# A cross-attention block on one core: q earlier and in halves, zero and constant rows by other queues

## The chip, the cores and the metric

The kernel runs on one NeuronCore of a Trainium2 chip. Its engines are TensorE (PE, matmul), VectorE (DVE), ScalarE (ACT), GpSimd (POOL) and SyncE (SP, which here only issues transfers). Two queues of DMAs are used, SP's (SPq, q1) and ACT's (ACTq, q10); their transfers run on the same 16 DMA engines. The metric is the time of one execution on the device in microseconds, lower is better, as the median of several runs. The profile is of one more execution; its times are counted from the start of its span.

## The reference

```python
# x [8,256,256], ctx [8,1601,256], mask all ones; D=256, H=16 heads of HD=16, INNER=1024
residual = hidden_states
x = layer_norm(hidden_states, ln1_w, ln1_b)
q = (x @ q_w + q_b)                      # by heads
k = (encoder_hidden_states @ k_w + k_b)  # by heads
v = (encoder_hidden_states @ v_w + v_b)  # by heads
scores = jnp.einsum('bhqd,bhkd->bhqk', q, k) * scale
scores = jnp.where(mask, scores, mask_value)
attn = jax.nn.softmax(scores, axis=-1)
out = jnp.einsum('bhqk,bhkd->bhqd', attn, v) ... @ cproj_w + cproj_b
hidden = out + residual
y = layer_norm(hidden, ln2_w, ln2_b)
y = gelu(y @ fc_w + fc_b) @ proj_w + proj_b
return hidden + y
```

## The kernel before

Each of the 8 batches has 256 queries and 1601 keys, padded to 13 key tiles of 128 (KT). The order of work is written out by hand, engine by engine, and every dependence is a semaphore.

Products that need full precision are done with each operand split in two parts, high and low, and three matmuls. The context of a batch arrives transposed in four chunks (cT, by `load_ctx`); ACT (in batch 0, `high`) or POOL (later, `c_high`) makes the high part c_hi, and POOL's `c_low` the low part c_lo. From these PE makes K in eight units, `k_unit(b, mt, c)`: mt is one of two groups of eight heads, c the chunk, six matmuls into the bank KB. DVE takes a unit out with two instructions (`k_evac`: kpart, high and low), and SP stores it in DRAM (`store_k`, k_scr). V is made in 13 units of six matmuls (`v_unit`) into the one bank XB, and DVE takes each out with one instruction (`v_evac`). The q path uses XB too: PE transposes the normalised x (`xt_unit`), DVE scales it (`xt_evac`), PE multiplies by the weights (`q_unit`), and DVE writes q, then its high and low part (`q_evac`), which SP stores (`store_q`, q_scr). XB has one occupant at a time, in the order of the list HEAD_X for batch 0.

The scores are computed from the tiles kst and qst, in four slots of four heads. A slot is filled back from DRAM by seven transfers (`fill`): three parts of K, three of q and the mask row (`fill_mask`). In kst, of every four rows three belong to the parts, and the fourth, MASKROW and its like, is zero or special: row 3 of each half is the mask row, row 63 of each half is constant. Batch 0 first has to clear kst (ACT copies zeros into it, eight instructions on line 656) and then write the constant rows, six transfers by SP (`constant_rows`, semaphore ones_in). `fill_ready` is what a fill waits for in batch 0: q stored, the K units of its group stored, the mask stored, the six constant transfers landed.

For a slot whose fill has landed (slot_in) PE makes products over a sample of keys (`max_unit`), DVE reduces them to row maxima and turns them (mrow), and SP writes them as a row of qst in four transfers (`send_rows`). Then PE can do the slot's scores (line 1145), ACT takes the exponential (line 602), and PE multiplies by V (line 1152). Before the first score PE has done all eight K units, the 13 V units, and the maxima of slots 0 and 1. From then on the loop over pairs of key tiles mixes the scores and value products of a batch with the K, V and q units of the next. An MLP over all tokens ends the kernel. A second path, computed in full when a check of the denominators fails, is not taken.

In the beginning the order on the queues is: SP loads w_kv, chunk 0, the x of four token tiles, chunks 1 and 2, w_qc, chunk 3, the rest of x; ACT loads the mask, the columns of biases and scales (cols_s), the rows of biases and the identity. ACT then waits for the columns, copies the mask as float and goes on to `high(0)`; DVE reduces the mask (`mask_rows`), then does the sums of x. PE's first matmul waits for c_lo of chunk 0 and the identity.

## Time and profile before

| | us |
|---|---|
| median of 3 runs | 750.32 (749.85 to 750.52) |
| the profiled execution | 747.24 |
| its span | 745.4 |
| PE busy in the span | 698.3 |
| ACT busy | 457.9 |
| DVE busy | 370.6 |
| POOL busy | 122.8 |

The page also has the 16 DMA engines busy at 0.9 or more of their time in the first slices of the span and at a third to two thirds in the middle, and a granted clock of PE that is below full only in the third slice and once later. How to read the rows below: a timeline has the start and the duration in us, the engine, the line, the instruction, what it writes and reads, the number of merged instructions, and in brackets how long the engine had been idle before it and what released it. A row of SPq or ACTq is the issuing of a transfer, not its data; how long after the issue the data had landed is a view of its own.

### The profile page before, as it was taken

To read this page: it belongs to the slowest core of one execution; us is meant where nothing else is said; L and a number is where in the kernel's file an instruction comes from. 1 tells how busy PE (TensorE), PEld (TensorE's weight loads), DVE (VectorE), ACT (ScalarE), POOL (GpSimd) and SP (SyncE) were. 2 spreads that over 40 slices of the span, in tenths; PEclk is the share of its full clock that TensorE was granted. 3 is DMA by queue.
4 is the path that set the end of the run, shared out by engine and by line. 5 is a ranking of instruction groups with operands and counts; after the bars stand their busy time and mean duration, and the time that the engine had idled before them with its cause. 6 is when DMAs were issued, how large, how long until landed. Compare 5 with 4: busy or idle time off the path is not lost.

```text
span 745.4 us, 16779 instructions
## 1 busy us (share of the span) xinstructions
PE 698.3 (94%) x7026; PEld 476.8 (64%) x7026; DVE 370.6 (50%) x824; ACT 457.9 (61%) x483; POOL 122.8 (16%) x90
## 2 busy tenths in 40 slices
PE   3679998999999999999999999999998978999997
PEld 3567665666566656665666566656664534697897
DVE  5655663554355535543555355525542322467663
ACT  5406568666865686568656865686566888633311
POOL 6222041003200320041003200410000600011010
PEclk9869999999999999999999999999999999999999
DMA  9677564356544653465346534654435500000000
GB/s 312 185 268 274 185 207 183 136 174 210 189 139 171 210 198 136 165 210 201 137 160 212 199 143 156 211 199 143 160 141 182 187 2 2 1 22 7 30 29 32
DMA packets 51081, 113.76 MB, mean 153 GB/s; under 512 B 6858, under 2 KB 39986, under 8 KB 49722
## 3 DMA queue, kind: packets, MB, share of 16 engines
q1 hardware_dynamic: 40488, 80.56, 31.9%
q10 hardware_dynamic: 10514, 32.08, 11.9%
q8 instruction: 58, 0.95, 0.5%
q14 instruction: 21, 0.17, 0.1%
HBM read 65.30 MB, written 47.06 MB: 151 GB/s over the span
## 4 chain that ended last, share of the span: by engine, by line
PE 77%; ACT 13%; issue 1%; DVE 1%; ACTq 0%; DVEq 0%
PE O L1152 22%; PE S L1145 16%; ACT pr L602 12%; PE XB L1082 11%; PE O L1082 10%; PE O L1239 6%; PE S L1082 6%; PE XB L1179 2%; PE MB L1132 2%; PE XB L1119 2%; PE XB L1111 0%; ACT pj_raw L610 0%; ACT L602 0%; PE O L1132 0%; DVE g_lo L921 0%
## 5 line engine op out<-in xcount | busy, mean ns | idle before, releaser
L602 ACT ACTIVATE pr<-S 128x1024 f32<-128x1024 f32 x416 | 400.6, 1024 | 176.6 <-PE S L1145 172.9
L1152 PE MATMUL O<-pr,vsl 128*17 128x256 f32 x3328 | 224.8, 384 | 1.3 <-DVE ot L816 1.3
L1145 PEld LDWEIGHTS S<-qst,kst 64*128 64x128 f32 x1664 | 116.0, 186 | 117.4 <-ACT pr L602 79.1
L1145 PE MATMUL S<-qst,kst 64*128 64x256 f32 x1664 | 170.5, 313 | 16.9 <-ACT pr L602 13.5
L1152 PEld LDWEIGHTS O<-pr,vsl 128*17 128x17 f32 x3328 | 74.9, 97 | 78.2 <-issue 16.4
L751 DVE TENSOR_SCALAR kpart<-O,cols_s 128x384 fp32r<-128x384 f32 x64 | 40.6, 635 | 120.4 <-PE O L1082 120.4
L526 POOL CAST c_hi<-cT 128x768 fp32r<-128x768 f32 (+1 forms) x28 | 23.9, 852 | 328.4 <-DMA cT<-in_ctx_t 202.9
L797 DVE TENSOR_REDUCE mx<-MB 128x2 fp32r<-128x512 f32 x64 | 44.1, 689 | 64.7 <-PE MB L1132 64.7
L1082 PE MATMUL XB<-w_hi,c_hi 128*128 128x256 f32 (+1 forms) x208 | 68.3, 328 | 2.6 <-DVE vsl L765 1.8
L765 DVE TENSOR_TENSOR vsl<-XB,rows_s 128x256 f32<-128x256 f32 (+1 forms) x104 | 43.3, 416 | 51.0 <-PE XB L1082 51.0
L1082 PE MATMUL O<-c_hi,w_hi 128*128 128x384 f32 (+1 forms) x128 | 52.8, 412 | 17.0 <-POOL c_lo L531 10.5
L531 POOL TENSOR_TENSOR c_lo<-cT,c_hi 128x768 fp32r<-128x768 f32 (+1 forms) x32 | 61.0, 1906 | 6.9 <-ACT c_hi L590 4.7
L1082 PE MATMUL XB<-w_lo,c_hi 128*128 128x256 f32 (+1 forms) x208 | 60.4, 290 | 0.0
L1082 PE MATMUL XB<-w_hi,c_lo 128*128 128x256 f32 (+1 forms) x208 | 60.1, 289 | 0.0
L620 ACT ACTIVATE g<-S,cols_s 128x512 f32<-128x512 f32 x32 | 22.1, 690 | 57.2 <-PE S L1082 52.9
L816 DVE STREAM_TRANSPOSE ot<-O 128x256 f32<-128x256 f32 x32 | 14.4, 450 | 76.4 <-PE O L1152 75.6
L1082 PEld LDWEIGHTS XB<-w_hi,c_hi 128*128 128x128 f32 (+1 forms) x208 | 40.1, 193 | 17.8 <-issue 9.4
L1082 PE MATMUL O<-c_lo,w_hi 128*128 128x384 f32 (+1 forms) x128 | 45.5, 355 | 0.0
L1082 PE MATMUL O<-c_hi,w_lo 128*128 128x384 f32 (+1 forms) x128 | 45.4, 355 | 0.0
L800 DVE TENSOR_REDUCE mx<-O 128x2 fp32r<-128x512 f32 x64 | 43.6, 681 | 0.0
L754 DVE SCALAR_TENSOR_TENSOR kpart<-O,cols_s,kpart 128x384 fp32r<-128x384 f32 x64 | 40.6, 635 | 2.3
L1082 PEld LDWEIGHTS O<-c_hi,w_hi 128*128 128x128 f32 x128 | 25.0, 195 | 26.2 <-issue 12.8
(101 smaller groups left out, 842.5 us busy)
## 6 DMA issues: line engine op xcount, KB each, us to landing
kst<-k_scr SPq DMA_DIRECT2D x89, 400.2 KB
k_scr<-kpart SPq DMA_DIRECT2D x48, 384.0 KB, 3.3
v_scr<-vsl ACTq DMA_DIRECT2D x8, 1768.0 KB, 6.0
cT<-in_ctx_t ACTq DMA_DIRECT2D x21, 384.0 KB, 5.0
k_scr<-kpart SPq DMA_DIRECT2D x16, 449.0 KB, 3.3
qst<-q_scr SPq DMA_DIRECT2D x87, 64.0 KB
q_scr<-qpart SPq DMA_DIRECT2D x16, 256.0 KB, 2.5
cT<-in_ctx_t ACTq DMA_DIRECT2D x7, 449.0 KB, 3.5
```

The lines of the kernel that those rows point to most:

```text
L526: nc.gpsimd.tensor_copy(c_hi[:, c, :, 0:n], cT[:, c, :, 0:n]).then_inc(hi_done, 1)
L531: nc.gpsimd.tensor_tensor(c_lo[:, c, :, 0:n], cT[:, c, :, 0:n], c_hi[:, c, :, 0:n].bitcast(F32), ALU.subtract).then_inc(lo_done, 1)
L602: nc.scalar.activation(pr[:, n % PBUF, :], S[:, 2 * (n % 2):2 * (n % 2) + 2, :] .rearrange("p a n -> p (a n)"), ACT.Exp).then_inc(s_.exp_d ...
L751: nc.vector.tensor_scalar(kpart[:, i, 0, 0:n], KB[:, 0:n], bk_s[:, mt:mt + 1], None, ALU.add).then_inc(kh_done, 1)
L754: nc.vector.scalar_tensor_tensor(out=kpart[:, i, 1, 0:n], in0=KB[:, 0:n], scalar=bk_s[:, mt:mt + 1], in1=kpart[:, i, 0, 0:n].bitcast(F32), ...
L765: nc.vector.tensor_tensor(vsl[0:m, b % 2, :, kt, :].rearrange("p s (h w) -> p s h w", w=VW)[:, :, :, 0:HD], XB[0:m, 0:D].rearrange("p (s h ...
L797: nc.vector.tensor_reduce(mx[:, s % 2, :, j], MB[:, :].rearrange("p (q k) -> p q k", q=QT), AX.X, ALU.max, negate=True).then_inc(mb_taken, 1)
L800: nc.vector.tensor_reduce(mx[:, s % 2, :, NJ + j], KB.rearrange("p (q k) -> p q k", q=QT), AX.X, ALU.max, negate=True).then_inc(kb_taken, 1)
L1082: last = nc.tensor.matmul(dst, a, c, start=i == 0, stop=i == len(terms) - 1)
L1145: last = nc.tensor.matmul(S[:, 2 * (n % 2) + g_, j * LQ:(j + 1) * LQ], kst[rows_, s, j, kt * P:(kt + 1) * P], qst[rows_, s, j, :], start=T ...
L1152: last = nc.tensor.matmul(O[32 * h:32 * h + VW, 0, 0:LQ], vsl[:, par, s, kt, h * VW:(h + 1) * VW], pr[:, n % PBUF, h * LQ:(h + 1) * LQ], s ...
L1239: last = nc.tensor.matmul(O[:, n % 2, 0:D], w[:, i, cut], v[:, i, :], start=i == 0 and m == 0, stop=i == NI - 1 and m == 2)
```

## The change

The units of q in batch 0 move forward: HEAD_X is now V0, the transposes, q, then V1 to V12; PE does the transposes between K units (0,1) and (0,2), q between (0,2) and (0,3), and V1 and V2 after (0,3). DVE follows, and `q_evac` works in halves by head group (mt), each with a semaphore and a store of its own (q_out[0], q_out[1]), so that slots 0 and 1 wait for the first half only. This halving holds for all batches.

kst is no longer cleared by eight ACT copies. POOL clears its last 63 columns, and one transfer on ACT's queue copies zeros from qst into every fourth row. The six constant rows are issued from ACT's queue, behind the contexts of batch 1. The four mask rows of batch 0 are written there before `fill_ready`; `fill` leaves them out in batch 0. The first part of x moves from SP's queue to ACT's, ahead of cols_s; the rest of x moves to ACT's queue, behind the contexts of batch 1. On DVE the sums of x come before the mask steps.

```diff
-HEAD_X = ["v0", "v1", "v2", "xt", "q"] + [f"v{t}" for t in range(3, KT)]
+HEAD_X = ["v0", "xt", "q"] + [f"v{t}" for t in range(1, KT)]
...
-            fill_mask(eng, s_, b, s)
+            if s_ is whole or b > 0:
+                fill_mask(eng, s_, b, s)
...
-            eng.wait_ge(q_out, 32 * (b + 1))
+            eng.wait_ge(q_out[s // 2], 16 * (b + 1))
             k_landed(eng, UK * b + CH * (s // 2 + 1))
             if b == 0:
-                eng.wait_ge(mask_out, 16)
                 eng.wait_ge(ones_in, 16 * 6)
...
             load_ctx(sp, 0, 0)
-            sp.dma_start(hid[:, 0:2 * QT, :], x[0:2 * QT].rearrange("n p d -> p n d")).then_inc(x_in, 16)
             load_ctx(sp, 0, 1)
             load_ctx(sp, 0, 2)
             sp.dma_start(w_qc_s[:], w_qc).then_inc(wqc_in, 16)
             load_ctx(sp, 0, 3)
-            sp.dma_start(hid[:, 2 * QT:TOK, :], x[2 * QT:TOK].rearrange("n p d -> p n d")).then_inc(xrest_in, 16)
...
-            for c in range(CH):
+            for c in range(CH - 1):
                 store_k(0, 0, c)
-            sp.wait_ge(pads_set, 3)
-            sp.wait_ge(kst_zeroed, SLOTS * NJ)
-            constant_rows()
-            store_q(0)
+            store_q_half(0, 0)
+            store_k(0, 0, CH - 1)
+            store_q_half(0, 1)
             fill_ready(sp, 0, 0)
             fill_k(sp, first, 0, 0, [0, 1])
...
             nc.gpsimd.memset(qst_d, 0.0).then_inc(pads_set, 1)
+            nc.gpsimd.memset(kst_d[:, :, :, LK:KP], 0.0).then_inc(pads_set, 1)
...
             act.dma_start(mk_u, mask).then_inc(mask_in, 16)
+            act.dma_start(hid[:, 0:2 * QT, :], x[0:2 * QT].rearrange("n p d -> p n d")).then_inc(x_in, 16)
             act.dma_start(cols_s[:], cols).then_inc(cols_in, 16)
...
             act.wait_ge(cols_in, 16)
             act.wait_ge(pads_set, 4)
+            act.dma_start(kst_d[MASKROW::PARTS].rearrange("p s j t -> p (s j) t"),
+                          qst_d[0:P // PARTS].rearrange("p s j q -> p (s j q)")[:, 0:KP].unsqueeze(1)
+                          .broadcast_to([P // PARTS, SLOTS * NJ, KP])).then_inc(kst_zeroed, 16)
...
-            zeros = qst_d.rearrange("p s j q -> p (s j q)")[:, 0:KP]
-            for s in range(SLOTS):
-                for j in range(NJ):
-                    nc.scalar.activation(kst[:, s, j, :], zeros, ACT.Copy).then_inc(kst_zeroed, 1)
             for c in range(CH):
                 next_ctx(1, c)
+            act.dma_start(hid[:, 2 * QT:TOK, :], x[2 * QT:TOK].rearrange("n p d -> p n d")).then_inc(xrest_in, 16)
+            act.wait_ge(kst_zeroed, 16)
+            constant_rows(act)
+            act.wait_ge(mask_out, 16)
+            for s in range(SLOTS):
+                fill_mask(act, first, 0, s)
             fill_ready(act, 0, 0)
             fill_k(act, first, 0, 0, [2])
             fill_q(act, first, 0, 0)
-            fill_mask(act, first, 0, 0)
...
                 for mt in range(2):
-                    last = nc.vector.tensor_scalar(qf[:, mt, :], XB[:, mt * LQ:(mt + 1) * LQ], bq_s[:, mt:mt + 1],
+                    if b > 0:
+                        dve.wait_ge(q_out[mt], 16 * b)
+                    step = nc.vector.tensor_scalar(qf[:, mt, :], XB[:, mt * LQ:(mt + 1) * LQ], bq_s[:, mt:mt + 1],
                                                    some[:, b:b + 1], ALU.add, ALU.mult)
...
+                    nc.vector.tensor_copy(qpart[:, mt, 0, :], qf[:, mt, :]).then_inc(qh_done, 1)
+                    dve.wait_ge(qh_done, 2 * b + mt + 1)
+                    nc.vector.tensor_tensor(qpart[:, mt, 1, :], qf[:, mt, :], qpart[:, mt, 0, :].bitcast(F32), ALU.subtract
+                                            ).then_inc(ql_done, 1)
```

Three places in the order of instructions follow. On PE, in the beginning, before: the last matmul of K unit (0,3) (128x450), the transposes of x, q, and the start of unit (1,0).

```order
L1082 MATMUL O<-c_hi,w_lo 128x450
L1111 MATMUL XB<-idn,xn 128x128 [waits xb_taken,xn_done]
L1111 MATMUL XB<-idn,xn 128x128 x3
L1119 MATMUL XB<-attT,w_qc_s 128x256 [waits xb_taken,wqc_in]
L1119 MATMUL XB<-attT,w_qc_s 128x256 x3
L1082 MATMUL O<-c_hi,w_hi 128x384 [waits kb_taken]
```

On PE now, from the transposes behind unit (0,1) to the start of unit (0,3):

```order
L1123 MATMUL XB<-idn,xn 128x128 [waits xb_taken,xn_done]
L1123 MATMUL XB<-idn,xn 128x128 x3
L1094 MATMUL O<-c_hi,w_hi 128x384 [waits kb_taken,lo_done]
L1094 MATMUL O<-c_lo,w_hi 128x384
L1094 MATMUL O<-c_hi,w_lo 128x384
L1094 MATMUL O<-c_hi,w_hi 128x384
L1094 MATMUL O<-c_lo,w_hi 128x384
L1094 MATMUL O<-c_hi,w_lo 128x384
L1131 MATMUL XB<-attT,w_qc_s 128x256 [waits xb_taken,wqc_in]
L1131 MATMUL XB<-attT,w_qc_s 128x256 x3
L1094 MATMUL O<-c_hi,w_hi 128x450 [waits kb_taken,lo_done]
```

The transposes and q have moved one and a half K units forward, and unit (0,3) now stands behind them. On ACT, the very first instructions before (pr is the mask's place, c_hi the context's high part):

```order
L583 DMA pr<-in_mask 8x1601
L584 DMA cols_s<-in_cols 128x20
L585 DMA rows_s<-in_rows 128x768
L586 DMA idn<-in_ident 128x128
L647 ACT_TABLE_LOAD [waits mask_in,pads_set]
L647 ACTIVATE pr<-pr 8x1601 [waits cols_in]
L590 ACTIVATE c_hi<-cT 128x2x384 [waits ctx_in0]
```

and now:

```order
L585 DMA pr<-in_mask 8x1601
L586 DMA hid<-in_x 128x4x256
L587 DMA cols_s<-in_cols 128x20
L588 DMA rows_s<-in_rows 128x768
L589 DMA idn<-in_ident 128x128
L650 DMA kst<-qst 32x8x1664 [waits pads_set,cols_in]
L655 ACT_TABLE_LOAD [waits mask_in]
L655 ACTIVATE pr<-pr 8x1601 [waits pads_set]
L593 ACTIVATE c_hi<-cT 128x2x384 [waits ctx_in0]
```

x stands ahead of the columns, and the wait for the columns stands ahead of the zeroing transfer and the table load. On ACT behind its last chunk of batch 0, before, up to the first fill:

```order
L590 ACTIVATE c_hi<-cT 128x900 [waits ctx_in3]
L656 ACTIVATE kst<-qst 128x1664 x8
L341 DMA cT<-in_ctx_t 128x2x384 [waits lo_done] x3
L341 DMA cT<-in_ctx_t 128x2x449 [waits lo_done]
L348 DMA kst<-k_scr 32x2x1601 [waits k_out3,k_out2,mask_out,k_out1,ones_in,k_out0,q_out]
L356 DMA qst<-q_scr 32x512 x3
L362 DMA kst<-mask_scr 2x2x1601
```

and now, up to the same fill:

```order
L342 DMA cT<-in_ctx_t 128x2x449 [waits lo_done]
L663 DMA hid<-in_x 128x12x256
L385 DMA kst<-ones 1x8x63 [waits kst_zeroed]
L387 DMA kst<-ones 1x104x128
L389 DMA qst<-ones 1x8x256
L385 DMA kst<-ones 1x8x63
L387 DMA kst<-ones 1x104x128
L389 DMA qst<-ones 1x8x256
L363 DMA kst<-mask_scr 2x2x1601 [waits mask_out]
L363 DMA kst<-mask_scr 2x2x1601 x3
L349 DMA kst<-k_scr 32x2x1601 [waits k_out2,k_out3,k_out1,ones_in,k_out0,q_out0]
L357 DMA qst<-q_scr 32x512 x3
```

The eight copies are gone, and the rest of x, the six constant rows and the four mask rows stand there.

## Rows read from the trace of the kernel before

**Rows 1.** The page, part 1: busy us, share of the span, instructions.

```profile
PE 698.3 (94%) x7026; PEld 476.8 (64%) x7026; DVE 370.6 (50%) x824; ACT 457.9 (61%) x483; POOL 122.8 (16%) x90
```

**Rows 2.** Busy by window: PE, PEld, DVE, ACT, POOL (instructions), PEclk, DMA share, GB/s.

```profile
140.00:221.00 81.00, 80.05 (x869) 52.18 (x862) 40.06 (x85) 53.89 (x57) 12.73 (x10) 1.00 0.49 168
```

**Rows 3.** Timeline of PE: the first maximum product and the first scores.

```profile
45.82 0.58 PE L1132 MATMUL MB<-kst,qst 63*128 63x256 f32 x1 [1.14 <-DMA kst<-mask_scr]
...
57.22 1.22 PE L1145 MATMUL S<-qst,kst 64*128 64x256 f32 x8
```

**Rows 4.** Timeline of SP's queue, 24 to 37 us (issues).

```profile
24.40 0.37 SPq L401 DMA_DIRECT2D k_scr<-kpart  x1
27.31 0.80 SPq L422 DMA_DIRECT2D kst<-ones  x1
...
32.01 0.95 SPq L407 DMA_DIRECT2D q_scr<-qpart  x2
36.38 1.57 SPq L348 DMA_DIRECT2D kst<-k_scr  x2
```

**Rows 5.** Timeline of ACT, the mask copy and the last four zeroing copies.

```profile
5.77 1.54 ACT L647 ACTIVATE pr<-pr 8x1601 f32<-8x1601 uint8 x1 [1.21 <-DMA cols_s<-in_cols]
...
21.21 6.01 ACT L656 ACTIVATE kst<-qst 128x1664 fp32r<-128x1664 f32 x4
```

**Rows 6.** DMA issues, first 25 us: queue, KB each, us to landing.

```profile
hid<-in_x SPq DMA_DIRECT2D x1, 512.0 KB, 7.5
...
cols_s<-in_cols ACTq DMA_DIRECT2D x1, 10.0 KB, 4.4
...
k_scr<-kpart SPq DMA_DIRECT2D x2, 384.0 KB, 6.0
...
k_scr<-kpart SPq DMA_DIRECT2D x1, 449.0 KB, 3.4
```

**Rows 7.** Timeline before the first exponential: row issues on SP, table load on ACT.

```profile
50.70 9.68 SPq L413 DMA_DIRECT2D qst<-mrow  x8
...
57.46 1.28 ACT L602 ACT_TABLE_LOAD   x1 [30.23 <-issue]
58.76 1.94 ACT L602 ACTIVATE pr<-S 128x1024 f32<-128x1024 f32 x2
```

**Rows 8.** Busy by window in the beginning, columns as in rows 2.

```profile
10.00:15.00 5.00, 3.61 (x13) 3.37 (x13) 4.83 (x18) 3.53 (x5) 2.21 (x2) 1.00 1.07 377
...
30.00:35.00 5.00, 1.95 (x6) 1.95 (x7) 3.29 (x4) 0.00 (x0) 1.26 (x1) 0.65 0.62 94
...
45.00:50.00 5.00, 4.18 (x19) 3.51 (x20) 2.83 (x6) 0.00 (x0) 1.60 (x2) 0.52 1.03 404
```

**Rows 9.** Timeline of POOL, the first low part of the context.

```profile
8.19 1.80 POOL L531 TENSOR_TENSOR c_lo<-cT,c_hi 128x768 fp32r<-128x768 f32 x1 [1.85 <-ACT c_hi L590]
```

**Rows 10.** Timeline of PE up to the first maximum.

```profile
10.13 0.66 PE L1082 MATMUL O<-c_hi,w_hi 128*128 128x384 f32 x1 [10.13 <-POOL c_lo L531]
...
14.93 0.66 PE L1082 MATMUL O<-c_hi,w_hi 128*128 128x384 f32 x1 [1.26 <-DVE kpart L754]
...
25.42 1.97 PE L1119 MATMUL XB<-attT,w_qc_s 128*128 128x256 f32 x8 [2.06 <-DVE attT L773]
...
33.05 0.69 PE L1082 MATMUL O<-c_hi,w_hi 128*128 128x384 f32 x1 [3.46 <-DVE kpart L754]
...
43.73 0.36 PE L1082 MATMUL XB<-w_hi,c_hi 128*128 128x256 f32 x1 [1.29 <-DVE vsl L765]
```

**Rows 11.** DVE: timeline; last, the subtraction of q in all batches (ns min/median/max).

```profile
7.34 1.81 DVE L709 TENSOR_REDUCE some_b<-pr 8x1 f32<-8x1601 f32 x1 [0.91 <-ACT pr L647]
...
11.62 1.33 DVE L729 BATCH_NORM_STATS2 st<-hid 128x6 f32<-128x256 f32 x4
...
13.51 0.62 DVE L751 TENSOR_SCALAR kpart<-O,cols_s 128x384 fp32r<-128x384 f32 x1
...
27.50 0.99 DVE L781 TENSOR_SCALAR xn<-XB,cols_s,some 128x256 f32<-128x256 f32 x2 [2.22 <-PE XB L1119]
...
L789 DVE TENSOR_TENSOR qpart<-xn,qpart x8: 691/693/2173, 29.6 to 524.3; 128x512 fp32r<-128x512 f32 x8
```

More of the change, by code:

```diff
@@ L271, in build @@
         k_out = [sem(f"k_out{i}") for i in range(KBUF)]
-        v_out, q_out = sem("v_out"), sem("q_out")
+        v_out = sem("v_out")
+        q_out = [sem(f"q_out{mt}") for mt in range(2)]
         mask_out, some_out, some_in, ones_in, mlpw_in, xagain_in = map(
@@ L379, in build, with constant_rows @@
         UK = 2 * CH
+        def constant_rows(eng):
+            for r0 in (0, HALF):
+                eng.dma_start(kst_d[r0 + MASKROW:r0 + MASKROW + 1, :, :, LK:KP].rearrange("p s j t -> p (s j) t"),
+                             ones[0:1, 0:KP - LK].unsqueeze(1).broadcast_to([1, SLOTS * NJ, KP - LK])).then_inc(ones_in, 16)
+                eng.dma_start(kst_d[r0 + MAXROW:r0 + MAXROW + 1, :, :, :].rearrange("p s j (n t) -> p (s j n) t", t=P),
+                             ones[1:2, 0:P].unsqueeze(1).broadcast_to([1, SLOTS * NJ * KT, P])).then_inc(ones_in, 16)
+                eng.dma_start(qst_d[r0 + MASKROW:r0 + MASKROW + 1, :, :, :].rearrange("p s j t -> p (s j) t"),
+                             ones[1:2, 0:LQ].unsqueeze(1).broadcast_to([1, SLOTS * NJ, LQ])).then_inc(ones_in, 16)
         def fill_ready(eng, b, s):
-            eng.wait_ge(q_out, 32 * (b + 1))
+            eng.wait_ge(q_out[s // 2], 16 * (b + 1))
             k_landed(eng, UK * b + CH * (s // 2 + 1))
             if b == 0:
-                eng.wait_ge(mask_out, 16)
                 eng.wait_ge(ones_in, 16 * 6)
@@ L638, in load_mlp @@
                 k_landed(act, UK * B)
-                act.wait_ge(q_out, 32 * B)
+                for mt in range(2):
+                    act.wait_ge(q_out[mt], 16 * B)
                 act.wait_ge(xb_taken, v_use(B - 1, KT - 1) + 1)
@@ L942, in head @@
                 v_evac(0, kt)
+            dve.wait_ge(x_in, 16)
+            for n in range(2 * QT):
+                x_stats(n)
+            x_moments(0, 2 * QT, 2 * QT)
             mask_rows()
@@ L948, in _ @@
             nc.vector.memset(att[:], 0.0).then_inc(att_zeroed, 1)
-            dve.wait_ge(x_in, 16)
-            for n in range(2 * QT):
-                x_stats(n)
-            x_moments(0, 2 * QT, 2 * QT)
             dve.wait_ge(cols_in, 16)
@@ L955, in _ @@
             k_evac(0, 0, 0)
+            newton(rs_rows(rs1, 0, 2 * QT), ln_steps, XA_VAR, ln_root, 1)
+            x_normalise(0)
             head(0)
             k_evac(0, 0, 1)
+            xt_evac(HEAD_X.index("xt"))
+            k_evac(0, 0, 2)
+            q_evac(0, HEAD_X.index("q"))
+            k_evac(0, 0, 3)
             head(1)
-            newton(rs_rows(rs1, 0, 2 * QT), ln_steps, XA_VAR, ln_root, 1)
-            k_evac(0, 0, 2)
             head(2)
-            x_normalise(0)
-            k_evac(0, 0, 3)
-            xt_evac(HEAD_X.index("xt"))
-            q_evac(0, HEAD_X.index("q"))
             for c in range(CH):
@@ L1248, in _ @@
             k_unit(0, 0, 1)
-            v_unit(0, 1)
+            xt_unit(0, HEAD_X.index("xt"))
             k_unit(0, 0, 2)
-            v_unit(0, 2)
-            k_unit(0, 0, 3)
-            xt_unit(0, HEAD_X.index("xt"))
             pe.wait_ge(wqc_in, 16)
             q_unit(HEAD_X.index("q"))
+            k_unit(0, 0, 3)
+            v_unit(0, 1)
+            v_unit(0, 2)
             for c in range(CH):
```

42 lines of the change are left out of this document (17 added, 25 removed).

## The prediction

> **What bounds the kernel now.** First the page: TensorE (PE) is busy for 94% of a span of 745.4 us [rows 1]. Then the busy times by window: in the steady stretch 140 to 221 us PE has 80.05 busy us of 81 [rows 2], so an edit there has to shorten PE's work, and this one adds or removes no matmul. What it can move is the moment at which the dense stretch begins. Next, PE's order in time at the beginning: the first maximum product starts at 45.82, after a wait for a DMA into the first K slot, and the first score products start at 57.22 [rows 3]. Behind 57.22 everything is packed, so what the first score gains or loses reaches the end one for one. The question is what sets 45.82, and what sets the 11.40 us from there to 57.22.
>
> What sets 45.82 is the chain of the first K slot. The queue of SyncE (SP) issues six constant rows from 27.31 on, then from 32.01 the two stores of q, and at 36.38 starts the slot's fill [rows 4]. The constant rows start at 27.31 because ScalarE (ACT) is at its eight zeroing copies until 27.22 [rows 5]; SP's last K store before them was issued at 24.40 [rows 4], so SP stood idle for 2.5 us. From 36.38 the slot needs 9.4 us until its product can run.
>
> **What the change removes there.** The eight ACT copies (the last four take 6.01 us [rows 5]) and with them SP's 2.5 us; six issues ahead of the q store on SP, 4.7 us (27.31 to 32.01), which go to ACT's queue; and one mask-row issue of about 0.6 us behind the slot's fills. The fill then waits for the latest of three landings: the constant rows, the first half of q, the store of K unit (0,3).
>
> **What it delays at the very start.** The 512 KB of x go onto ACT's queue ahead of the columns. The columns landed 4.4 us after their issue at 1.39, so at 5.8; x took 7.5 us on SP's queue [rows 6]. ACT's mask copy, at 5.77 before [rows 5], waits for the columns, and the table load (1.28, as at 57.46 [rows 7]) and the issue of the zeroing transfer now stand behind the same wait. Bounds: columns at 5.8 if x does not hold them up, near 9 if x takes what it took on SP. With half of 377 GB/s [rows 8], 524 KB of x are 2.8 us, from about 4: I take 6.8. Then: issue 0.6, table load 1.28, mask copy 1.54 [rows 5], c_hi 0.88 and c_lo 1.80 [rows 9], handovers 0.2. The first matmul starts at 13.1 where it was 10.13 [rows 10], 2.9 late (1.9 at the lower end, 5 at the upper). Part of it has a cover: the second K unit waited for VectorE (DVE) until 14.93 [rows 10]. DVE's mask steps and clears took 4.3 us (7.34 to 11.62 [rows 11]); behind a mask copy that ends at 10.2 they end at 14.6, and the x sums, 1.9 us, now run ahead of them in DVE's idle time. PE ends the first unit at 15.1, its evacuation takes 1.28 (twice 0.62 and a gap [rows 11]), and the second unit starts at 16.5: 1.6 late.
>
> The Trainium skill, DMA: Bandwidth & Descriptors, "Queues, rings and completion order", says that each DMA engine consumes the descriptors of a queue in ring order. By that rule the columns can't pass x, the lower end is out, and the first matmul is later than 12.0. No run here shows it yet.
>
> **The chain from the second K unit to the fill.** DVE now does the Newton steps, the two normalisations and V0 (0.95, 0.73 and 0.41, 2.1 in all) and evacuates unit (0,1) by 19.9. Unit (0,2) runs 20.0 to 21.6, the evacuation of xT beside it. q's products take 1.97 [rows 10], to 23.6. q is then taken out in halves: 0.5 (0.99 for both [rows 11]), then copy and subtraction; the whole subtraction has a median of 0.69 and was 2.17 the first time [rows 11], so a half costs 1.2 in all by the median and 2 by the longest. I take 1.2, since the shortest and the median agree (691 and 693 ns). The first half can be stored at 24.8, the second is done at 26.0, and unit (0,3) is evacuated by 27.4; its store goes out at 27.5 where it was 24.40 [rows 4]. Such stores took 3.4 to 6.0 us to land [rows 6]: 31 to 33.5.
> The constant rows: ACT issues them behind the next context and the rest of x, from about 20.5, for 4.7 us; four mask rows follow. They queue behind 1.5 MB of x and 1.6 MB of context. The beginning also moves 1.70 MB of zeros (32 partitions x 8 x 1664 x 4 bytes), at 377 GB/s [rows 8] 4.5 us of DMA time that did not exist, so the traffic that ended at 27 ends at 31.5, and the rows, 2 us of slow transfers, land at 33.5. That is the last of the three: the fill starts at 33.5, 2.9 earlier than 36.38. With 9.4 less 0.6 the slot is ready at 42.3.
>
> **PE's own work up to there.** V1 and V2 now stand behind q and unit (0,3). V2 ends at 28.7, unit (1,0) at 29.9, and unit (1,1) starts at 31.3 instead of 33.05: the 3.46 us hole before it [rows 10] is split up, not removed. From (1,1) to V7, at 43.73 [rows 10], were 10.7 us, half of it at the lower clock. So V7 starts at 42.0, or at 40.2 with the higher clock throughout, and PE is ready for the maximum at 41 to 43. I take 42.5 for the maximum, 3.3 us earlier than 45.82.
>
> **From the maximum to the scores.** The 11.40 us ran at 1.2 GHz (0.52 granted in 45 to 50), as did most of 30 to 35 behind the hole [rows 8]. Nothing edited stands in it. Two other things end near 57.22: the row DMAs of the first slots, issued from 50.70 at 1.2 us each, four for a slot, and ACT's issuing of slot 2, behind which it loads its table at 57.46 and starts the exponential at 58.76 [rows 7]. Both follow from events that move with the maximum, so I leave 11.40 and price the stretch at nothing; if PE had the higher clock there, these two would keep the further gain to 1 or 2 us. In the steady part q leaves by six DVE instructions instead of four, about 0.15 us in each of seven batches, with DVE busy 40.06 us of 81 [rows 2]: no cost on PE.
>
> **Sum.** The profiled execution took 747.24 us, 745.4 of it span; less 3.3 it is 743.9. The median of the timed runs is 750.32, 3.1 above the profiled one; the same 3.3 off it gives 747.0.
>
> **Rivals.** A: PE keeps the higher clock and the slot is ready at 41: the maximum 4.5 earlier and 1.5 to 2.5 less behind it, 743.4 to 744.4. For it: the 3.46 us hole, behind which the clock was low, becomes holes of 1 to 2. Against: V7 had waited 1.29 [rows 10] and the maximum 1.14 [rows 3] when the clock fell a second time, and such waits come again.
> B, slower: the constant rows hold up the first slot. They are many short writes into single partitions; with the queue nearly empty they still kept the fill from 27.31 to 36.38 together with q. Behind ACT's backlog, which ends at 31.5, and without overlap of issue and landing, 7.5 us put them at 39.0, slot 0 at 47.8 and the time at 752.3. It decides against the change from a fill start of 37.3. Against it: 4.7 of those us were issuing, which now overlaps the backlog.
> C, no change: the slot is early, but PE at the lower clock from unit (1,1) on, or from a start at the upper end (columns at 9, 2 us more), reaches the maximum at 44.5 to 45.5; or slot 2 and the rows gate the scores where they did: 749 to 750.3.
> By one more rule of the Trainium skill (the same page, "Rules for kernel authors") a transfer whose outermost size is 2 runs on at most two DMA engines. The mask row is one, and it is what the wait before 45.82 names [rows 3]; by the rule its landing leaves the chain as well as its issue, which points to A.
>
> **How the numbers follow.** Forecast (745.5 to 748.5) 0.45; A, or faster still, 0.22; C 0.20; B 0.13. A measurement of this kernel tells about 0.2%, 1.5 us, from no change. Forecast and A lie beyond that; C is within it; B's nearer end is within it too: faster 0.68, same 0.20, slower 0.12. The range takes in A and C whole and leaves out B beyond its first part: 743.2 to 751.2.
>
> **What would show each step.** ACT's mask copy ends near 10.2 and the first matmul is near 13; the hole before unit (1,1) is under 2 us; the fill starts at 33.5; the first maximum is at 42.5 and the first scores at 54. It is wrong if the columns land after 8, if the first maximum still waits for a DMA at 45 or later, or if the stretch from maximum to scores is not 11.4.

## The result: 0.96% slower

| | median, us | lowest to highest | runs |
|---|---|---|---|
| before | 749.72 | 746.38 to 750.52 | 6 |
| changed | 756.51 | 753.18 to 761.23 | 6 |

The ratio is 1.0096, 95% interval 1.0055 to 1.0136. The forecast was 747.0 with a range up to 751.2, faster: the time is outside the range and on the other side of the kernel before. The profiled execution took 753.18 us with a span of 751.3; that of before had 747.24 and 745.4 [the table of before], so the trace shows 5.9 us of the loss.

The middle of the kernel is what it was. Busy by window, columns as in rows 2, of the changed kernel, which answers to [rows 2]:

```profile
140.00:221.00 81.00, 80.06 (x875) 52.12 (x877) 40.29 (x91) 54.18 (x57) 13.15 (x10) 1.00 0.54 185
```

80.06 busy us of PE against 80.05, and DVE only 0.23 us busier for its longer q. The loss is in the beginning. Timeline of PE after, with the places of [rows 10] and [rows 3]:

```profile
15.62 0.66 PE L1094 MATMUL O<-c_hi,w_hi 128*128 128x384 f32 x1 [15.62 <-POOL c_lo L533]
...
19.44 0.66 PE L1094 MATMUL O<-c_hi,w_hi 128*128 128x384 f32 x1 [0.28 <-DVE kpart L763]
...
23.54 0.96 PE L1123 MATMUL XB<-idn,xn 128*128 128x128 f32 x4 [2.44 <-DVE vsl L774]
...
26.77 2.06 PE L1131 MATMUL XB<-attT,w_qc_s 128*128 128x256 f32 x8
...
53.79 0.36 PE L1094 MATMUL XB<-w_hi,c_hi 128*128 128x256 f32 x1 [1.29 <-DVE vsl L774]
54.67 0.39 PE L1144 MATMUL MB<-kst,qst 63*128 63x256 f32 x1
...
64.62 0.74 PE L1157 MATMUL S<-qst,kst 64*128 64x256 f32 x8
```

The first scores come at 64.62 where they came at 57.22, 7.4 us later; the first exponential is 6.4 us later (65.16 against 58.76), the end 5.9. The first maximum, at 54.67, no longer waits for a DMA. It waits for PE's own work, and that work waited here, on DVE (timeline around q):

```profile
27.67 0.62 DVE L763 SCALAR_TENSOR_TENSOR kpart<-O,cols_s,kpart 128x384 fp32r<-128x384 f32 x1
35.44 0.54 DVE L792 TENSOR_SCALAR xn<-XB,cols_s,some 128x256 f32<-128x256 f32 x1 [7.16 <-DMA some<-some_scr]
```

DVE stands still for 7.16 us, all but the first half microsecond of them with q finished in XB (26.77 and 2.06), because the factor `some` (one number for each batch from the mask's maximum, spread to all partitions by a trip through DRAM) has not come back. Everything that DVE and PE have behind q waits too: unit (0,3) is not taken out, and V1 can't have XB. SP's queue shows the trip; its rows answer to [rows 4]:

```profile
16.40 0.36 SPq L441 DMA_DIRECT2D some_scr<-some_b  x1
...
29.58 0.36 SPq L444 DMA_DIRECT2D some<-some_scr  x1
...
36.80 0.37 SPq L416 DMA_DIRECT2D q_scr<-qpart  x1
39.36 0.37 SPq L411 DMA_DIRECT2D k_scr<-kpart  x1
...
43.09 1.54 SPq L349 DMA_DIRECT2D kst<-k_scr  x2
```

The store of a few bytes goes out at 16.40 and has landed only at 29.58; the load back takes until 35.4. The chain that ended last, read up to 70 us (start, duration), names both:

```profile
1.86 7.22 DMA cols_s<-in_cols
...
14.66 1.65 DVE pr L720
16.40 13.16 DMA some_scr<-some_b
29.58 5.84 DMA some<-some_scr
35.44 0.55 DVE xn L792
```

What kept a tiny store for 13 us is seen in the windows (columns as in rows 2; they answer to the first of [rows 8]) and in the DMA issues of the first 30 us:

```profile
10.00:15.00 5.00, 0.00 (x0) 0.00 (x0) 2.60 (x7) 4.97 (x5) 1.33 (x1) 1.00 1.08 270
15.00:20.00 5.00, 4.10 (x14) 3.87 (x15) 3.98 (x11) 2.35 (x4) 5.00 (x4) 1.00 0.98 118
20.00:25.00 5.00, 2.34 (x11) 1.69 (x10) 4.86 (x10) 0.00 (x0) 3.13 (x2) 0.87 0.98 107
```

```profile
kst<-qst ACTq DMA_DIRECT2D x1, 1664.0 KB, 19.1
```

From 15 to 25 us the DMA engines are occupied for 0.98 of their time and move 107 to 118 GB/s. The zeroing transfer, issued at 9.10, is what they work on: it lands after 19.1 us, at 28.2, and the small store 1.4 us behind it. By queue, nothing at all moves on SP's in these 10 us (packets, MB, share of the 16 engines):

```profile
q10 hardware_dynamic: 180, 1.13, 98.1%
```

SP issues in order, so the wait for the small store also holds up the K stores behind it: they go out from 29.98, in the kernel before from 18.86.

### The profile page after: what moved, and what is told of

The parts are those of the page before. It is cut to its first block, busy times and chain, and to the rows that moved or that the text cites. A ratio compares the mean times of both kernels' runs of the same rounds, so it can differ in the third digit from the quotient of the medians.

```text
span 751.3 us, 16781 instructions
## 1 busy us (share of the span) xinstructions
PE 694.1 (92%) x7026; PEld 473.7 (63%) x7026; DVE 374.4 (50%) x840; ACT 445.8 (59%) x475; POOL 123.8 (16%) x91
## 4 chain that ended last, share of the span: by engine, by line
PE 77%; ACT 13%; DVE 4%; DMA 3%; issue 2%; ACTq 0%; DVEq 0%
PE O L1164 21%; PE S L1157 16%; ACT pr L605 12%; PE XB L1094 11%; PE O L1094 10%; PE O L1251 6%; PE S L1094 6%; PE XB L1191 2%; PE XB L1131 2%; DMA some_scr<-some_b 2%; PE MB L1144 2%; DMA cols_s<-in_cols 1%; DMA some<-some_scr 1%; DVE kpart L760 1%; DVE kpart L763 0%
## 5 line engine op out<-in xcount | busy, mean ns | idle before, releaser
L1157 PE MATMUL S<-qst,kst 64*128 64x256 f32 x1664 | 169.5, 311 | 17.1 <-ACT pr L605 13.7
L1094 PE MATMUL O<-c_lo,w_hi 128*128 128x384 f32 (+1 forms) x128 | 45.5, 355 | 0.0
```

Source lines behind the costliest of these rows:

```text
L1094: last = nc.tensor.matmul(dst, a, c, start=i == 0, stop=i == len(terms) - 1)
L1157: last = nc.tensor.matmul(S[:, 2 * (n % 2) + g_, j * LQ:(j + 1) * LQ], kst[rows_, s, j, kt * P:(kt + 1) * P], qst[rows_, s, j, :], start=T ...
```

## The experiments

The theory to be tested: the zeroing transfer is slow because of where it reads. It takes its zeros from the partitions 0 to 31 of qst; written to every fourth partition of kst they are 1.70 MB. The rivals: 1.70 MB more are too much for this stretch whatever their source (volume), or the start is what costs (x ahead of the columns, which makes all of it later), or making q early is itself no gain. In each comparison the kernel before ran in turn with the experiment on the same chip; its medians there were 748.63, 748.05 and 748.15. The changed kernel was not run again in these turns, so it is compared with the experiments by its ratio. c_src64 was run once, for its profile. The table holds the ratio with its interval and, from one profiled execution each, the start of the first matmul, of q on DVE, of the first slot's fill on SP, of the first maximum and of the first scores.

| kernel | ratio | matmul | q | fill | maximum | scores |
|---|---|---|---|---|---|---|
| before | | 10.13 | 27.50 | 36.38 | 45.82 | 57.22 |
| changed | 1.0096 (1.0055 to 1.0136) | 15.62 | 35.44 | 43.09 | 54.67 | 64.62 |
| a_spread | 1.0022 (1.0000 to 1.0044) | 15.33 | 28.77 | 38.29 | 47.40 | 57.99 |
| c_src64 | one run, 750.49 us | | 30.56 | 40.43 | 49.10 | 60.70 |
| a_actzero | 0.9995 (0.9964 to 1.0027) | 13.42 | 27.88 | 37.12 | 46.98 | 56.23 |
| a_cols | 1.0090 (1.0054 to 1.0126) | 12.27 | 34.00 | 43.10 | 53.51 | 63.42 |
| a_spread_cols | 1.0046 (1.0022 to 1.0069) | 12.29 | 30.33 | 39.95 | 48.57 | 59.70 |
| s_xfirst | 1.0011 (0.9976 to 1.0045) | 13.81 | 29.86 | 37.14 | 47.43 | 58.36 |
| b_start | 0.9987 (0.9954 to 1.0020) | 10.32 | 26.09 | 35.88 | 43.78 | 55.42 |
| b_qonly | 1.0034 (0.9998 to 1.0070) | 10.40 | 26.98 | 39.90 | 49.32 | 58.85 |
| b_restlate | 1.0022 (1.0002 to 1.0043) | 10.32 | 27.18 | 39.19 | 47.69 | 59.09 |
| b_qlast | 1.0034 (1.0007 to 1.0061) | 10.38 | 30.17 | 37.89 | 49.18 | 59.15 |

### a_spread: the same transfer from every fourth partition

The changed kernel with one edit; bytes, number of rows and destination stay.

```diff
-                          qst_d[0:P // PARTS].rearrange("p s j q -> p (s j q)")[:, 0:KP].unsqueeze(1)
+                          qst_d[0::PARTS].rearrange("p s j q -> p (s j q)")[:, 0:KP].unsqueeze(1)
```

> The changed kernel with one edit: the transfer of zeros reads every fourth partition of qst instead of partitions 0 to 31; same bytes, same place in the queue. Theory S (the 32 neighbouring source partitions limit the rate, 107 GB/s from 13 to 25 us at a DMA share near 1): the zeros move at 300 GB/s or more and land 8 to 10 us after their issue instead of 19.1, the small store of the mask's maximum lands within 4 us instead of 13.2, DVE's wait of 7.2 us before q goes, the first scores start near 57 instead of 64.6, and the time is 747 to 750. Theory V (any 1.7 MB on ACT's queue at this time does it, or SBUF to SBUF is slow as such): landing still 17 to 19 us, the wait 5 to 7, time 755 to 758.

749.31 us (748.30 to 753.50). By the ratios that is 5.5 us less than the changed kernel, and the two intervals do not meet. Windows, DMA issue and SP's queue of this kernel:

```profile
13.00:16.00 3.00, 0.67 (x2) 0.70 (x3) 2.96 (x3) 2.97 (x5) 2.61 (x2) 1.00 1.01 424
15.00:20.00 5.00, 4.38 (x15) 4.15 (x16) 3.97 (x11) 2.06 (x4) 5.00 (x4) 1.00 0.78 238
```

```profile
kst<-qst ACTq DMA_DIRECT2D x1, 1664.0 KB, 8.2
```

```profile
16.12 0.36 SPq L441 DMA_DIRECT2D some_scr<-some_b  x1
...
18.49 0.36 SPq L444 DMA_DIRECT2D some<-some_scr  x1
```

424 GB/s from 13 to 16 us at the same share of busy time, again with nothing on SP's queue; the transfer landed after 8.2 us instead of 19.1, the small store in under 2.4 instead of 13.2, and q leaves at 28.77 with no wait for `some`. The volume is the same, so the volume is not the cause. The first matmul moves only from 15.62 to 15.33, so the start has next to nothing to do with the 6.6 us that the first scores gain.

### c_src64: every second partition of the lower half

```diff
-                          qst_d[0:P // PARTS].rearrange("p s j q -> p (s j q)")[:, 0:KP].unsqueeze(1)
+                          qst_d[0:2 * P // PARTS:2].rearrange("p s j q -> p (s j q)")[:, 0:KP].unsqueeze(1)
```

> The changed kernel with the source of the zeros at partitions 0, 2, 4 to 62. It tells what about partitions 0 to 31 is slow. If it is that four neighbouring partitions are read by two DMA engines at once, this source is fast: above 300 GB/s, as with every fourth. If it is that only half of the partition space is read, the rate stays at 100 to 220 GB/s in 13 to 25 us, with the landing of the zeros 12 to 19 us after the issue.

Windows of this kernel, and the DMA issue:

```profile
15.00:20.00 5.00, 4.02 (x14) 3.79 (x15) 3.98 (x11) 2.54 (x4) 5.00 (x4) 1.00 1.00 211
```

```profile
kst<-qst ACTq DMA_DIRECT2D x1, 1664.0 KB, 13.3
```

211 GB/s at a share of 1.00, twice the 107 of the changed kernel and half the 424 of a_spread. That is the slower of the two outcomes in the expectation: spreading the 32 partitions over half of the partition space does not make the source fast. 32 partitions are read in all three kernels. One reading that fits is the number of groups of four neighbouring partitions in which they lie: 8, 16 and 32, as the rates stand 1 to 2 to 4. The step and the extent of the source differ as well, no run parts them from the groups, and 424 may be the limit of the DMA engines. The small store follows in every case behind the zeros: these land at 28.2, 22.5 and 17.1, and SP could issue the load of `some` at 29.58, 22.75 and 18.49.

The Trainium skill, SBUF — State Buffer, "Door 1: The DMA port swizzle", says that the bandwidth of a DMA depends on how many of 16 ports its partitions reach; by its table the partitions 0 to 31 and 0 to 62 reach the same eight and every fourth reaches all. It points the right way for a_spread. It does not give the factor of two between the other two sources, and there the measurement decides: the count of ports alone is not enough.

### a_actzero: the eight ACT copies back, no zeroing transfer

```diff
-            act.dma_start(kst_d[MASKROW::PARTS].rearrange("p s j t -> p (s j) t"),
-                          qst_d[0:P // PARTS].rearrange("p s j q -> p (s j q)")[:, 0:KP].unsqueeze(1)
-                          .broadcast_to([P // PARTS, SLOTS * NJ, KP])).then_inc(kst_zeroed, 16)
...
             for c in range(2, CH):
                 high(c)
+            zeros = qst_d.rearrange("p s j q -> p (s j q)")[:, 0:KP]
+            for s in range(SLOTS):
+                for j in range(NJ):
+                    nc.scalar.activation(kst[:, s, j, :], zeros, ACT.Copy).then_inc(kst_zeroed, 1)
```

> The changed kernel with the zeroing undone: ACT clears kst with its eight copies, behind the last chunk of batch 0, as before; everything else of the change stays. Both theories: the DMA engines are free of the zeros, the mask's maximum lands within 3 us of 16.8, DVE has no wait for it before q, the low rate between 13 and 28 us is gone. The copies take 12 us from about 17.5, so the constant rows start at 30 and the fill at 36 to 37: first maximum at 46, first scores at 56 to 58, time 749 to 752. If it stays at 756, the zeros are not the cause.

749.5 us (746.86 to 754.05), no measurable difference from before, as expected. With this the loss is undone a second way, without any transfer of zeros: the small store lands in 2.6 us (14.21 to 16.81) and q does not wait for `some`. The zeros no longer wait ahead of the table load and the mask copy, so the first matmul is at 13.42. The fill starts at 37.12, later than before in spite of the early q. The removed copies were not what stood between the kernel and a gain.

### a_cols and a_spread_cols: the columns ahead of x

The x of four token tiles goes behind the columns, the rows and the identity on ACT's queue, in the changed kernel and in a_spread.

```diff
             act.dma_start(mk_u, mask).then_inc(mask_in, 16)
-            act.dma_start(hid[:, 0:2 * QT, :], x[0:2 * QT].rearrange("n p d -> p n d")).then_inc(x_in, 16)
             act.dma_start(cols_s[:], cols).then_inc(cols_in, 16)
             act.dma_start(rows_s[:], rows.partition_broadcast(P)).then_inc(rows_in, 16)
             act.dma_start(idn[:], ident).then_inc(idn_in, 16)
+            act.dma_start(hid[:, 0:2 * QT, :], x[0:2 * QT].rearrange("n p d -> p n d")).then_inc(x_in, 16)
```

> The changed kernel with x behind the columns, rows and identity on ACT's queue. It tells the price of the columns behind x: they land at 5.5 to 6 instead of 9.1, the mask copy starts at 8 instead of 11.25, the first matmul at 12 instead of 15.6. Theory S and V: the zeros are then issued 3 us earlier and end 3 us earlier, but still hold the store of the mask's maximum to their end, so 2 to 3.5 us gained: 752 to 755. A rival, that the start sets everything: 749 or less.

> The changed kernel with both edits: zeros from every fourth partition, and x behind the columns, rows and identity. If the two costs are apart, this is the prediction's own picture with a better start: first matmul at 12, no wait for the mask's maximum, fill start at 31 to 33, first scores at 53 to 55, time 743 to 747. If the zeros are slow as such (V), 752 to 755, as with the second edit alone.

754.79 us (753.16 to 756.69) and 751.37 us (747.98 to 755.68). The columns land in 4.3 us instead of 7.2 and the first matmul comes at 12.27, 3.35 earlier, but nothing of it reaches the end. DVE does the sums of x first, and x now lands 11.1 us after its issue at 2.77. So the mask steps are late. SP's queue in a_cols:

```profile
19.66 0.36 SPq L441 DMA_DIRECT2D some_scr<-some_b  x1
...
28.41 0.36 SPq L444 DMA_DIRECT2D some<-some_scr  x1
```

Its store of `some` goes out 3.3 us later than in the changed kernel, and q leaves at 34.00, still after a wait of 5.08 us for `some`. In a_spread_cols the same store goes out at 19.76, and q, at 30.33, waits 1.31, but for PE's products. My expectation for a_spread_cols had the start's gain added to that of the source. It was wrong: the second edit moved the late thing from the columns to x, which heads DVE's order.

### s_xfirst: what the late start costs by itself

The kernel before with two moves: x on ACT's queue ahead of the columns, and DVE's sums of x ahead of the mask steps.

```diff
+            act.dma_start(hid[:, 0:2 * QT, :], x[0:2 * QT].rearrange("n p d -> p n d")).then_inc(x_in, 16)
             act.dma_start(cols_s[:], cols).then_inc(cols_in, 16)
...
-            sp.dma_start(hid[:, 0:2 * QT, :], x[0:2 * QT].rearrange("n p d -> p n d")).then_inc(x_in, 16)
...
+            dve.wait_ge(x_in, 16)
+            for n in range(2 * QT):
+                x_stats(n)
+            x_moments(0, 2 * QT, 2 * QT)
             mask_rows()
```

> The kernel before with only the start of the change: x on ACT's queue ahead of the columns, and DVE's sums of x ahead of its mask steps. Columns at 9 instead of 5.8, first matmul at 13.4 (the table load is not behind the columns here), 3.2 us late. If what is behind follows one for one, first scores at 60 and 751 to 752. If the slot's chain (constant rows behind ACT's copies) covers it, first maximum at 46 to 47.5 and the time within 1 to 1.5 us of the kernel before.

748.58 us (747.00 to 754.62), no measurable difference. The first matmul is 3.7 us later and the first scores 1.1 us. The constant rows start at 27.48 as they did (27.31 in [rows 4]). Behind them SP now waits 2.1 us for q and issues its stores at 34.22 instead of 32.01; these land in 2.3 us instead of 3.6, and the fill starts 0.8 us later. So the order of before absorbs most of a late start.

### b_start: the early q with the start of before

The changed kernel with the spread source, x back on SP's queue, DVE's mask steps first, and the zeroing transfer behind `high(1)`.

```diff
-            act.dma_start(kst_d[MASKROW::PARTS].rearrange("p s j t -> p (s j) t"),
-                          qst_d[0:P // PARTS].rearrange("p s j q -> p (s j q)")[:, 0:KP].unsqueeze(1)
-                          .broadcast_to([P // PARTS, SLOTS * NJ, KP])).then_inc(kst_zeroed, 16)
...
+            act.dma_start(kst_d[MASKROW::PARTS].rearrange("p s j t -> p (s j) t"),
+                          qst_d[0::PARTS].rearrange("p s j q -> p (s j q)")[:, 0:KP].unsqueeze(1)
+                          .broadcast_to([P // PARTS, SLOTS * NJ, KP])).then_inc(kst_zeroed, 16)
             x_root(0, 2 * QT, XA_VAR)
```

> The changed kernel with two parts mended: zeros read from every fourth partition and issued behind the second high part of the context, and the start as in the kernel before (x on SP's queue behind chunk 0, mask steps of DVE ahead of the sums of x). What is left of the change is q early and in halves, constant and mask rows on ACT's queue, the rest of x late. Theory: the start alone cost 5 us (first matmul 15.33 with spread zeros against 10.13), so here the first matmul is at 10.2, the first maximum near 43, the first scores near 53.5 and the time 745 to 747 against 748.6. Rival: the slot's fill does not follow the start (K stores and constant rows in a full queue), first maximum at 45 or later and the time within 1 us of the kernel before.

747.73 us (745.01 to 751.04): no measurable difference from before. It has the lowest ratio of all versions, but the interval overlaps those of several others. Its timelines show why the early q brings so little. PE and DVE first:

```profile
20.35 1.09 PE L1123 MATMUL XB<-idn,xn 128*128 128x128 f32 x4 [3.93 <-DVE vsl L774]
```

```profile
15.09 1.56 DVE L728 TENSOR_TENSOR rs<-rs 128x4 f32<-128x4 f32 x1
16.69 2.00 DVE L730 TENSOR_TENSOR rs<-rs 128x4 f32<-128x4 f32 x1
...
18.93 0.16 DVE L734 TENSOR_TENSOR rs<-rs 128x4 f32<-128x4 f32 x1
```

The Newton steps, on four numbers for each partition, take 0.16 us when POOL is idle and 1.56 and 2.00 beside POOL's `c_low` (two of it, from 14.80 to 18.67). In the order of before they came when `c_low` was done. They make a hole of 3.93 us on PE. Then SP and the last steps of ACT:

```profile
30.01 1.61 SPq L411 DMA_DIRECT2D k_scr<-kpart  x1
...
35.88 1.55 SPq L349 DMA_DIRECT2D kst<-k_scr  x2
```

```profile
31.13 3.84 ACTq L363 DMA_DIRECT2D kst<-mask_scr  x4
```

q's first half is stored at 27.45, but K unit (0,3), which now stands behind q, is stored at 30.01 and lands 5.7 us later, and the mask rows on ACT end at 34.97. The fill starts at 35.88, 0.5 us earlier than before. The fill, however, is not what the first maximum waits for here:

```profile
33.89 0.44 PE L1094 MATMUL O<-c_hi,w_hi 128*128 128x384 f32 x1 [0.73 <-DVE kpart L763]
...
42.91 0.36 PE L1094 MATMUL XB<-w_hi,c_hi 128*128 128x256 f32 x1 [1.29 <-DVE vsl L774]
...
43.78 0.39 PE L1144 MATMUL MB<-kst,qst 63*128 63x256 f32 x1
```

The maximum follows V7 without a wait. Unit (1,1), at 33.89, is even later than the 33.05 of before [rows 10]; what is gained comes behind it, where PE has a granted clock of 1.00 from 30 to 45, against 0.65 and 0.67 before from 30 to 40. The first scores come 1.8 us earlier, with a granted clock of 0.50 ahead of them, from 50 to 55. Even so they are not what starts the dense stretch. The chain that ended last, read up to 66 us, goes another way:

```profile
42.46 9.81 DMA k_scr<-kpart
...
52.45 0.56 ACTq L349
...
56.28 1.28 ACT L605
57.58 1.95 ACT pr L605 x2
```

The store of the last K unit, (1,3), needs 9.8 us to land. Only then can ACT issue its six transfers of slot 2, load its table and start the first exponential, at 57.58, while the scores have stood ready since 55.42. That is 1.2 us earlier than 58.76 [rows 7]. In the kernel before, the same store went out at 43.28 and landed in 9.5 us. The early q does not shorten this path, which is the same in a_spread (9.2 us), a_actzero (9.8) and b_qonly (12.6).

### b_qonly: the kernel before with nothing but the early q in halves

PE's and DVE's order, HEAD_X, `q_evac` and the halves of the store as in the changed kernel. Start, zeros by ACT and constant rows by SP as before. Its SP block reads:

```diff
-            for c in range(CH):
+            for c in range(CH - 1):
                 store_k(0, 0, c)
+            store_q_half(0, 0)
+            store_k(0, 0, CH - 1)
+            store_q_half(0, 1)
             sp.wait_ge(pads_set, 3)
             sp.wait_ge(kst_zeroed, SLOTS * NJ)
             constant_rows()
-            store_q(0)
```

> The kernel before with only the q part of the change: q between K units (0,2) and (0,3), taken out in halves, stores in the order unit (0,2), first half, unit (0,3), second half, then the wait for ACT's eight copies and the constant rows as before. Theory: the hole before K unit (1,1) shrinks from 3.5 to under 2 us and PE is ready for the maximum at 42 to 43, but the constant rows still start behind the copies and behind unit (0,3), so the fill starts at 35 to 37 and the first maximum stays at 44 to 46: same time within 1.5 us. If q early were itself the loss, 751 or more.

751.45 us (749.41 to 759.16); the interval of the ratio just takes in no change. The constant rows stand behind the store of unit (0,3) on SP, which is later for the early q (30.91 instead of 24.40), so they are issued from 31.91 instead of 27.31 and the fill starts at 39.90, 3.5 us later than before. The expectation, 35 to 37, had the rows behind that store too, but not how late both would be. The median lies where the early q was to be "itself the loss"; by the ratio a loss is not shown, a gain is ruled out beyond 0.02%.

### b_restlate and b_qlast: two tries at the fill

b_restlate is b_start with the rest of x (1.5 MB) behind the mask rows on ACT's queue. b_qlast is b_restlate with q behind unit (0,3), on PE, DVE and SP.

```diff
-            act.dma_start(hid[:, 2 * QT:TOK, :], x[2 * QT:TOK].rearrange("n p d -> p n d")).then_inc(xrest_in, 16)
             act.wait_ge(kst_zeroed, 16)
             constant_rows(act)
             act.wait_ge(mask_out, 16)
             for s in range(SLOTS):
                 fill_mask(act, first, 0, s)
+            act.dma_start(hid[:, 2 * QT:TOK, :], x[2 * QT:TOK].rearrange("n p d -> p n d")).then_inc(xrest_in, 16)
```

```diff
             xt_unit(0, HEAD_X.index("xt"))
             k_unit(0, 0, 2)
+            k_unit(0, 0, 3)
             pe.wait_ge(wqc_in, 16)
             q_unit(HEAD_X.index("q"))
-            k_unit(0, 0, 3)
```

> The version with the start of before and the spread zeros (b_start), with one more move: the 1.5 MB of the rest of x are issued on ACT's queue behind the mask rows instead of ahead of the constant rows. There the constant rows' first issue took 4.29 us and the last 3.62 us, and the K(0,3) store, issued at 30.01, took 5.7 us to land, so the fill started at 35.88. Theory (the fill is gated by traffic of x that nobody needs yet): the constant rows are issued from 19.1 to 24, the mask rows by 26.5, the K(0,3) store lands in 3.5 to 4 us, the fill starts at 33.5 to 34; the first maximum then waits for PE's own work (V7 at 42.9) and comes at 43 to 43.8, so that 0 to 0.8 us are gained: 746.5 to 748. Rival (the moved x delays the first fills instead, issued in the same queue directly ahead of them): the fill's K part waits behind x, the first maximum comes at 45 or later, 749 to 750.

> As b_restlate, with q behind K unit (0,3) instead of ahead of it, on PE, DVE and SP; V1 and V2 stay behind both. Theory (the later K(0,3) store, 27.5 forecast and 30.0 measured, took from the first fill what the earlier q gave it): K(0,3) is stored at 28.5, q's halves from 29.5, landing by 33 to 34; the fill starts at 33.5 to 34.5 as in b_restlate and the time is the same within 1 us. Rival (the order of the two matters): with the Newton steps stalled beside POOL, PE has work in K(0,3) to do while DVE evacuates xT, and the hole of 3.93 us before the transposes is the only one left: V7 comes 1 us earlier and the time is 1 us shorter than b_restlate.

749.80 us (745.79 to 753.40) and 750.80 us (747.96 to 757.96), 12 runs each: both slightly slower than before, by 0.2 and 0.3%, with intervals just clear of 1. For b_restlate the time and the late maximum of the rival came, but not by its way: the fill itself started late. The constant and mask rows are indeed issued by 29.70, 5.3 us earlier than in b_start. But x then moves during the store of unit (0,3). DMA issues of b_restlate:

```profile
hid<-in_x ACTq DMA_DIRECT2D x1, 1536.0 KB, 9.7
...
k_scr<-kpart SPq DMA_DIRECT2D x1, 449.0 KB, 7.9
```

The store, issued at 31.11, takes 7.9 us instead of 5.7, the fill starts at 39.19 (SP waits 6.9 us for it), and the first maximum waits 2.74 us for a DMA at 47.69. b_qlast's fill starts at 37.89 and its first maximum comes at 49.18: here PE is late, since q leaves DVE only at 30.17 and V1 to V12 wait behind it. Neither beats the kernel before, and by b_start's chain an earlier fill had little to give.

## Why the prediction was wrong

**The bytes of the zeros were priced at the wrong rate.** "At 377 GB/s [rows 8] 4.5 us of DMA time" took the rate of loads from DRAM into all partitions for a transfer inside SBUF out of 32 neighbouring ones. It moved at 107 to 118 GB/s and landed after 19.1 us. That is the failed term of the sum. a_spread shows its share: the ratio falls from 1.0096 to 1.0022, 5.5 of 7.2 us, and the first scores come 6.6 of 7.4 us earlier.

**A wait was left out.** The slow transfer alone would have cost DMA time; it cost path time because q waits for `some`. SP's queue in the kernel before shows the same trip:

```profile
10.92 0.35 SPq L439 DMA_DIRECT2D some_scr<-some_b  x1
...
18.46 0.36 SPq L442 DMA_DIRECT2D some<-some_scr  x1
```

The store had 7.5 us and the load had landed by 22.4, 5 us before q was taken out at 27.50 [rows 11], so no wait named it. The prediction listed the mask steps as work of DVE, moved them by 3 us with the mask copy and brought q forward by 3 to 4, and never asked what else q needs. With the two it would have found the slack gone. In a_spread, with the trip short again, the wait is gone.

**The start.** Columns 6.8: they landed at 9.1 (issue at 1.86 and 7.2), after x, which had landed at 8.4 (1.41 and 7.0). Half the rate for x was the wrong middle, the upper bound of 9 the right value; the first matmul was at 15.62 instead of 13.1. By the ring-order rule of the Trainium skill, DMA: Bandwidth & Descriptors, "Queues, rings and completion order", the columns can't pass x, and the trace agrees. Of the price, "1.6 late" after the cover of the second unit: that unit came at 19.44 where 16.5 was forecast. s_xfirst shows that such a delay costs little in the order of before (1.1 us of 3.7 at the first scores). In a_spread the first scores are 0.8 late behind a start 5.2 late.

**The Newton steps.** 0.95 us for them was read where POOL was idle. Moved forward they ran beside `c_low`: 0.42 and 2.03 us for two instructions that take 0.16, and the transposes waited 2.44 us. q's products ended at 28.8 where 23.6 was forecast, of which the start makes 2.9.

**What was right.** The halves of q cost 1.25 us each (35.44 to 36.69), 1.2 was taken. DVE's six instructions in the steady part cost PE nothing. The fill was indeed set by the three landings that were named, but the last of them was the K store, in the changed kernel (2.6 us of SP's wait) as in b_start (3.1), and not the constant rows. These were issued from 28.20 and not from 20.5: ACT spent 8.57 us on three context transfers behind the zeros, where a_spread took 0.37 to 0.39 us for each, waiting for POOL between them, and had its constant rows from 22.57. Rival B had nearly this place for the constant rows and its sign, with 752.3 (its threshold of 37.3 should be 37.0, 45.82 less 8.8); but it is not shown right. The maximum didn't wait for the fill: PE's V7 began at 53.79 and the maximum followed it without a wait for a DMA. The hole before unit (1,1) is under 2 us, as forecast (0.30 us before 44.79), but one of 7.3 us stands before V1 at 37.37. That the mask row no longer ends the wait for the slot fits the rule of the same page, "Rules for kernel authors", on outermost size 2, but it is also issued earlier, and no run parts the two.

**The gain itself.** Without the failed terms (b_start: old start, fast zeros) the fill is 0.5 us earlier, not 2.9, since K(0,3) pays for the early q, at 30.01 instead of the forecast 27.5. PE's own path was mis-sized too: unit (1,1) starts at 33.89, not at 31.3, and the first maximum, at 43.78 instead of 42.5, follows PE and not the fill. The first scores are 1.8 us earlier, not 3.3. The last step failed with them: the prediction left the table load and slot 2 aside, since both "follow from events that move with the maximum". Slot 2 hangs on the landing of K(1,3), 9.8 us behind its issue, and that sets the first exponential, 1.2 us earlier. The time is the same within its interval, 0.9954 to 1.0020, which would also hide a gain of 1.2 or 1.8 us. So b_start ends where rival C put it, with slot 2 as the gate; C's maximum at 44.5 to 45.5 did not come. From the maximum to the scores were 11.64 us, as the 11.40 left untouched; in the changed kernel it was 9.95, with the clock at 1.00 from 45 to 60, the part of rival A that held.

**What stays open.** Why the source's spread sets the rate was not followed further than the three points. Where the last 0.5 us between the first exponential (6.4 late) and the end (5.9 late) were recovered is not known. Nor is it shown that what the first scores gain reaches the end one for one, as the prediction had it: a_actzero's profiled execution has its scores 1.0 us earlier than before and its span 6.0 us longer, and a single execution can't tell such a gain from scatter. The changed kernel's medians lie 3.3 above its profiled execution; single runs of all these kernels scatter by up to 1%, so differences of the experiments below some 0.3% rest on the intervals alone.

## What to carry to other kernels

Price a transfer by a row that reads and writes the same kind of places; here bytes over the rate of another kind were wrong by more than three times, and while such a transfer occupied the engines, a few bytes on another queue waited with it. When a step is moved forward, list all its operands and follow each back to its source: the one that had slack in the old order has no row with a wait. What stands behind the moved step in every queue in order (here K(0,3) on DVE and SP) pays for it, and may be what the consumer waits for next. Before pricing an earlier arrival, follow every path into the first step of the dense stretch: here the exponential hung on the last K store and slot 2, and not on the scores.

## What the hardware showed that was not expected

- A copy inside SBUF out of 32 partitions, 1664 KB, landed in 19.1 us from the partitions 0 to 31, in 13.3 from every second of 0 to 62, in 8.2 from every fourth, beside other transfers each time. While it had the engines to itself, the rates were 107, 211 and 424 GB/s with the engines equally busy.
- A store of a few bytes on SP's queue took 13.2, 6.3 and 2.4 us in these three kernels, and landed 1.4, 0.3 and 1.4 us after the other queue's transfer. In the kernel before, without such a transfer but with the engines full of loads (1.07 from 10 to 15), it took 7.5; in a_actzero 2.6.
- A DVE instruction on 128x4 elements took 1.56 to 2.03 us beside a POOL tensor operation and 0.16 without it. The Trainium skill, SBUF — State Buffer, "Who interferes with whom", says that DVE and GpSimd share a pair of ports under an exclusive lock, and that a DVE instruction with two SBUF inputs contends with a GpSimd instruction that reads SBUF. The rows agree: 2.0 us is about the length of one such POOL operation (1.80 in [rows 9]), and the reciprocal ahead of them, with one input, took 0.17 beside POOL (14.89 in b_start).
- Six small issues of the constant rows took 4.7 us on SP's queue [rows 4]; on ACT's they took 4.7 (a_spread_cols), 5.6 (a_spread), 10.5 (changed) and 11.0 us (b_start, 20.12 to 31.09), with single issues between 0.6 and 4.29. All four had 1.5 MB of x directly ahead of them in the queue, so that alone does not set it, and no run shows what does.
